# Attention scores built by a transfer through DRAM and VectorE instead of by TensorE

## The reference, cut to what matters

```
first branch (once):   h = x' @ W_fc^T ; f1 = h.a1 ; f2 = h.a2
    s[i,j] = leaky_relu(f1[i] + f2[j], 0.2), -1e9 where adj[i,j] == 0
    out = elu(softmax_j(s) @ x')
second branch (3 layers), mask = adj + eye > 0:
    si = x @ attn_w[l,:256] ; sj = x @ attn_w[l,256:]
    s[i,j] = leaky_relu(si[i] + sj[j] + attn_b[l], 0.2), -inf where not mask
    h = layernorm(x + softmax_j(s) @ x) * g1 + beta1
    x = layernorm(h + gelu(h @ W1 + b1) @ W2 + b2) * g2 + beta2      (W1 256x1024, W2 1024x256)
```

## Time and profile before

| | |
|---|---|
| median of 3 runs | 2795.41 us (2794.3 to 2795.49) |
| the profiled execution | 2794.51 us, of it span 2792.7 us |
| busy share of the span | TensorE 96%, its weight loads 86%, VectorE 82%, ScalarE 77%, GpSimd 61% |
| mean granted TensorE clock | 0.981 of full |
| DMA | 201.34 MB, mean 72 GB/s; queue 1 holds 21.8% of 16 engines' span |

### The profile page before, as it was taken

One profiled execution on the slowest core, in us unless ns is written; L12 is line 12 of the kernel. 1 busy time (PEld: TensorE's weight loads), 2 busy tenths in 40 slices (PEclk: granted clock), 3 DMA queues, 4 the chain that ended last, 5 costly groups with the idle time before them and its releaser, 6 DMA issues.

```text
span 2792.7 us, 53529 instructions
## 1 busy us (share of the span) xinstructions
PE 2668.0 (96%) x16868; PEld 2390.7 (86%) x16868; DVE 2301.8 (82%) x8507; ACT 2147.8 (77%) x3982; POOL 1692.1 (61%) x2197
## 2 busy tenths in 40 slices
PE   3599999999999999999999999999999999999997
PEld 2388989898888898898888898989888999999997
DVE  5999888889888888888888888888988777777774
ACT  4588888878787878787877787878777876776774
POOL 4656655656766565666666665655666644544655
PEclk7599999999999999999999999999999999999999
DMA  6221122212222221222221212121323111111111
GB/s 188 93 75 54 65 76 65 71 61 86 83 96 69 66 73 52 80 65 83 79 97 59 80 65 76 56 80 45 102 80 99 54 52 52 35 52 52 50 63 53
DMA packets 118014, 201.34 MB, mean 72 GB/s; under 512 B 12736, under 2 KB 85472, under 8 KB 117728
## 3 DMA queue, kind: packets, MB, share of 16 engines
q1 hardware_dynamic: 117728, 197.87, 21.8%
HBM read 113.95 MB, written 83.89 MB: 71 GB/s over the span
## 4 chain that ended last, share of the span: by engine, by line
PE 70%; DVE 14%; POOL 7%; issue 5%; ACT 3%; DMA 0%; DVEq 0%; POOLq 0%; SPq 0%; ACTq 0%
PE bank L569 33%; PE bank L554 26%; PE ps_u L528 5%; DVE g_lo L917 3%; DVE st L891 3%; POOL xo L358 3%; PE ps_u L610 2%; PE ps_s L523 2%; POOL rs L1198 2%; DVE ub L972 1%; POOL hb L358 1%; DVE ub L1002 1%; PE ps_s L515 1%; DVE vb L886 1%; ACT g_hi L792 1%
## 5 line engine op out<-in xcount | busy, mean ns | idle before, releaser
L569 PE MATMUL bank<-w_hi,g_hi 128*128 128x256 f32 x3072 | 891.7, 290 | 19.0 <-DVE g_lo L917 18.2
L569 PE MATMUL bank<-w_hi,g_lo 128*128 128x256 f32 x3072 | 865.0, 282 | 0.0
L569 PE MATMUL bank<-w_lo,g_hi 128*128 128x256 f32 x3072 | 863.6, 281 | 0.0
L792 ACT ACTIVATE g_hi<-bank,b_eff 128x512 fp32r<-128x512 f32 x768 | 529.0, 689 | 432.8 <-PE bank L554 427.4
L917 DVE TENSOR_TENSOR g_lo<-bank,g_hi 128x512 fp32r<-128x512 f32 x768 | 517.7, 686 | 178.3 <-ACT bank L794 165.7
L554 PE MATMUL bank<-zt_hi,w_hi 128*128 128x512 f32 x1536 | 646.6, 421 | 7.1 <-DVE g_lo L917 3.7
L554 PE MATMUL bank<-zt_hi,w_lo 128*128 128x512 f32 x1536 | 607.1, 395 | 0.0
L554 PE MATMUL bank<-zt_lo,w_hi 128*128 128x512 f32 x1536 | 606.1, 395 | 0.0
L569 PEld LDWEIGHTS bank<-w_hi,g_hi 128*128 128x128 f32 x3072 | 578.5, 188 | 30.5 <-DVE g_lo L917 29.2
L569 PEld LDWEIGHTS bank<-w_lo,g_hi 128*128 128x128 f32 x3072 | 579.1, 189 | 0.8
L569 PEld LDWEIGHTS bank<-w_hi,g_lo 128*128 128x128 f32 x3072 | 578.3, 188 | 0.0
(11 more groups left out here) (95 smaller groups left out, 4291.7 us busy)
## 6 DMA issues: line engine op xcount, KB each, us to landing
xb<-x_scratch SPq DMA_DIRECT2D x88, 512.0 KB, 4.0
x_scratch<-xo SPq DMA_DIRECT2D x64, 512.0 KB, 4.8
xin<-in_x SPq DMA_DIRECT2D x40, 512.0 KB, 4.6
r_scratch<-elu_r SPq DMA_DIRECT2D x32, 512.0 KB, 3.1
xin<-r_scratch SPq DMA_DIRECT2D x32, 512.0 KB, 4.6
out<-xo SPq DMA_DIRECT2D x32, 512.0 KB, 3.3
m<-m_scratch SPq DMA_DIRECT2D x96, 128.0 KB, 3.7
x_scratch<-h SPq DMA_DIRECT2D x24, 512.0 KB, 2.9
```

The costliest lines, as they stand in the source:

```text
L569: mm = pe.matmul(y, g[:, c, r * P:(r + 1) * P], w[:, l, c, :], start=(c == 0 and n == 0), stop=(c == C - 1 and n == 2))
L792: act.activation(g_hi[:, c, :], block_in, ACT.Gelu, bias=bias).then_inc(g_hi_ready, 1)
```

## The change

For steps from 0 on (`by_memory(s)`), scores no longer pass TensorE. When the dots of a unit are there, SP writes the column `dots[:, 1, :]` to a small DRAM tensor `s2_u` (each element a piece of its own), waits for it, and reads it back as one row of 512 values broadcast over the 128 partitions, straight into `e1` (`e0` for the first branch). VectorE adds the mask and takes the row maximum in one fused instruction per graph, whose output stays in `e1`. ScalarE makes its exponentials from `e1`, one into PSUM and one in place. In steps below 0 the old way stays.

With it come moves: on VectorE `next_biases` goes from behind `first_variance` to behind `g_low(5)`, `input_statistics`, `second_statistics`, `low_rows` and the variances to behind `g_low(7)`; on TensorE `turns` goes from ahead of `second(3)` to behind it; waits on `scores_ready` become waits on `cc_ready`; some semaphores count by other numbers.

```diff
# SP, head of body
+                if by_memory(s) and v1 is not None:
+                    sp.wait_ge(dots0_ready, 2 * T * st.nth0(v1))
+                    sp.wait_ge(masks0_ready, st.nth0(v1))
+                    sp.dma_start(s2_u[2].rearrange("t n -> n t"), dots0[:, 1, :],
+                                 allow_slow_non_contiguous=True).then_inc(s2_0_out, 16 if v1 > V0 else 16 * (V0 + 1))
+                    sp.wait_ge(s2_0_out, 16 * st.nth0(v1))
+                    if v1 <= CH:
+                        sp.wait_ge(et0_ps, st.nth0(v1 - 1))
+                    sp.dma_start(e0.rearrange("p t m -> p (t m)"),
+                                 s2_u[2].rearrange("t n -> (t n)").partition_broadcast(P)).then_inc(s2_0_in, 16 if v1 > V0 else 16 * (V0 + 1))
...
-                        sp.wait_ge(scores_ready, st.nth(s + 1))
+                        sp.wait_ge(cc_ready if by_memory(s - 1) else scores_ready, st.nth(s + 1))
# SP, behind the store of m_new, ahead of the store of elu_r and the load of xin
+                if by_memory(s + 1) and live(s + 3):
+                    sp.wait_ge(dots_ready, st.nth(s + 3, 2 * T))
+                    sp.dma_start(s2_u[(s + 3) % 2].rearrange("t n -> n t"), dots[(s + 3) % 2][:, 1, :],
+                                 allow_slow_non_contiguous=True).then_inc(s2_out, 48 if s + 3 == 2 else 16)
+                    sp.wait_ge(m_in, 16 * st.nth(s + 3))
+                    sp.wait_ge(s2_out, 16 * st.nth(s + 3))
+                    sp.wait_ge(et_ps, st.nth(s + 3))
+                    sp.dma_start(e1.rearrange("p t m -> p (t m)"),
+                                 s2_u[(s + 3) % 2].rearrange("t n -> (t n)").partition_broadcast(P)).then_inc(s2_in, 16)
# TensorE, steps from 0 on
                 hidden(1)
-                next_scores()
                 first_turn()
                 hidden(2)
                 hidden(3)
-                first_scores()
...
                 second(2)
+                second(3)
                 turns()
-                second(3)
# ScalarE, exponentials
+                    if in_e:
+                        act.activation(src, e[:, t, :], ACT.Exp, bias=cols[:, 1, t:t + 1], scale=SLOPE)
+                        a = act.activation(e[:, t, :], e[:, t, :], ACT.Exp, bias=cols[:, 0, t:t + 1])
# VectorE, branch_biases (the scalar step now comes first)
-                dve.tensor_reduce(sm[:, 0, :], scores.rearrange("p (t m) -> p t m", t=T), AX, ALU.max)
+                if mask is None:
+                    ins = dve.tensor_reduce(sm[:, 0, :], scores, AX, ALU.max)
+                else:
+                    for t in range(T):
+                        ins = dve.tensor_tensor_reduce(scores[:, t, :], scores[:, t, :], mask[:, t, :], 1.0, LOWEST,
+                                                       ALU.add, ALU.max, sm[:, 0, t:t + 1])
# VectorE, order of steps from 0 on
                 g_low(1)
                 first_variance()
-                next_biases()
                 g_low(2)
                 first_norm()
                 g_low(3)
-                input_statistics()
                 g_low(4)
                 g_low(5)
+                next_biases()
+                g_low(6)
+                g_low(7)
+                input_statistics()
                 second_statistics()
-                g_low(6)
+                low_rows()
                 second_variance()
-                g_low(7)
                 input_variance()
                 if v1 is not None and early_step(v1) >= 0:
                     mask_sums(v1)
-                low_rows()
                 input_shift()
# GpSimd, first_mask
-                            pool.wait_ge(scores0_ready, st.nth0(v0 - 1))
+                            pool.wait_ge(cc0_ready if by_memory(s) else scores0_ready, st.nth0(v0 - 1))
```

More of the change, by code:

```diff
@@ L18 @@
 BIG = 2.0 ** 100
+LOWEST = -3.0e38
 class Step:
@@ L207, in build @@
         m_in = sem("m_in")
+        s2_out = sem("s2_out")
+        s2_in = sem("s2_in")
+        s2_0_out = sem("s2_0_out")
+        s2_0_in = sem("s2_0_in")
         m_out = sem("m_out")
@@ L450, in body @@
                         sp.dma_start(xb[(s + 3) % 2][:, :, :],
-                                     pick(xs_u, st, layer(s + 3) * G + group(s + 3))).then_inc(x_in, 16)
+                                     pick(xs_u, st, layer(s + 3) * G + group(s + 3))).then_inc(x_in, 16 if s + 3 > CH else 16 * (CH - 2))
                 if live(s - 2):
@@ L583, in next_scores @@
                 def next_scores():
-                    if live(s + 2):
+                    if live(s + 2) and not by_memory(s):
                         pe.wait_ge(dots_ready, st.nth(s + 2, 2 * T))
@@ L596, in first_scores @@
                 def first_scores():
-                    if v1 is not None:
+                    if v1 is not None and not by_memory(s):
                         pe.wait_ge(dots0_ready, st.nth0(v1, 2 * T))
@@ L628, in turns @@
                         pe.wait_ge(e_ready, st.nth(s + 2))
-                        turn_weights(ps_s, e1, et_ps)
+                        turn_weights(ps_s, e1, et_ps, 2 if s + 2 == 0 else 1)
                 if s < 0:
@@ L918, in g_low, with masked, mask_of @@
                                           ALU.subtract).then_inc(g_lo_ready, 1)
+                def masked(e, scores):
+                    return e[:, :, :] if by_memory(s) else scores.rearrange("p (t m) -> p t m", t=T)
+                def mask_of(m):
+                    return m if by_memory(s) else None
                 def first_biases():
                     if v1 is not None:
[L922 to L923 removed]
+                        if by_memory(s):
+                            dve.wait_ge(s2_0_in, 16 * st.nth0(v1))
+                        else:
+                            dve.wait_ge(scores0_ready, st.nth0(v1))
+                        branch_biases(st.nth0, v1, masked(e0, ps_s0), mask_of(m0), small0, dots0, cc0, None, max0_steps, cc0_ready)
                 junk = ub if s >= 0 else vb
@@ L988, in next_biases @@
                     if live(s + 2):
-                        dve.wait_ge(scores_ready, st.nth(s + 2))
+                        if by_memory(s):
+                            dve.wait_ge(s2_in, 16 * st.nth(s))
+                        else:
+                            dve.wait_ge(scores_ready, st.nth(s + 2))
                         if live(s + 1):
@@ L992, in next_biases @@
                         l2 = layer(s + 2)
-                        branch_biases(st.nth, s + 2, ps_s, small, dots[s % 2], cc, ab_col[:, l2:l2 + 1], max_steps,
+                        branch_biases(st.nth, s + 2, masked(e1, ps_s), mask_of(m1[s % 2]), small, dots[s % 2], cc, ab_col[:, l2:l2 + 1], max_steps,
                                       cc_ready)
```

32 lines of the change are left out of this document (19 added, 13 removed).

## The result

The change makes the kernel slower: 3237.86 us median of 4 runs (3234.14 to 3242.39) against 2794.88 of the kernel before on the same chip, ratio 1.158 (95% interval 1.157 to 1.160), +443 us. The forecast had the sign right and the size wrong: 2985 us, range up to 3050.

A forecast was written before the change was run, and what follows sets the result against it. TensorE was taken to bound C and the light steps, VectorE A. Periods of A, B, C gave 154 us, the residual-sum root 13, light steps 24: 191 on 2794.5, so 2985 us, own range 2900 to 3050, stated range 2775 to 3050.

The forecast's parts named there:

- the sign: Whole kernel: slower given 0.75, same 0.07, faster 0.18.
- A: Step s mod 3 = 2, input rows of a new group and norm of an older one: 27.35 to 32.3 us, +4.9.
- B: Step s mod 3 = 0, middle stage of the first branch: 26.9 to 27.4 us, +0.5.
- C: Step s mod 3 = 1, late stage of the first branch: 29.4 us, +1.0.
- the locks: Biases on VectorE beside GpSimd's hb, each operation waiting for a GpSimd instruction: 3.0 us per step, bounds 0 and 3.7.
- Rival 1: Fused operations don't lock against hb: about 2782 us; 0.07 as no change, 0.18 for faster together with another rival.
- light step: One of the 20 last steps, without first branch, bound by TensorE and a link: 26.2 to 27.4 us, +1.2.
- uncovered root in A: VectorE's input_shift follows the variances directly and waits for two roots on GpSimd: 1.5 us.
- Cost 0: SP's write of the dots and the broadcast land well before the biases, 12 us into the step: no cost.
- rival 4: Transfers land later than 12 us; 5 us more would make over 3200 us; chance 0.03.
- TensorE has no idle time at all: In the 20 last steps of 26.22 us TensorE never idles, so it bounds them.
- the 80 of the prediction: Score rows taken off TensorE, 121 x 0.66 = 80 us, the most the change can give.

The follow-up runs named there:

- e1: Kernel after without the 4-byte writes of the dots to DRAM and their waits, broadcasts reading a constant row: 3107.3 us.
- e3: Kernel after without the 4-byte writes (broadcast of a constant row) and with GpSimd's scaled rows (hb) behind the biases: 2935.7 us.
- e7: Kernel after with dots written as 128 pieces of 16 bytes and e1, e0 laid out node by graph, computation complete: 3160.7 us.
- e10: Kernel before with only the statistics, low rows and variances moved behind g_low(7), biases at their old place: 2939.5 us.
- e5: e3 with the turn of the weights again ahead of second(3) on TensorE: 3028.5 us.
- e6: e4 with the turn of the weights again ahead of second(3) on TensorE: 3045.0 us.
- e13: Kernel before without the four transposes of the score rows, the mask's matmul alone writing the bank: 2771.1 us, ratio 0.9915.
- e2: Kernel after with GpSimd's scaled rows (hb) made to wait until the biases of the same step are done: 3070.3 us.
- e4: Kernel after with its orders kept, but scores made by TensorE as before and no transfers through DRAM: 2945.3 us.
- e9: Kernel before with only next_biases moved behind g_low(5) in the steady state: 3097.3 us.
- e12: Kernel after with 16-byte pieces, kernel before's order on VectorE and TensorE, own broadcast tile, first branch left on TensorE: 2835.7 us, ratio 1.0146.

## Why the prediction was right or wrong

**Where the forecast went.** The profiled execution grew by 439 us. Against the forecast, by kind of step: the first five 45 (forecast 0), 23 A 131 (24 A: 118), 23 B 139 (25), 23 C 73 (24), the last 20 steps 51 (24). A came out; B is the largest miss.

**Right: the sign and the locks; A with some luck.** Rival 1 (no locks) is refuted. The pitch of 0.74 us for a held operation, worked out from the dots of a prologue step, is what the trace has (median 0.743 us), though fewer than half of the operations are held. Forecast for locks: 3.0 us of VectorE per step, of which 2.6 came (biases 4.3 us in e1, 1.7 in e3). Measured as a part of the total: 172 us (e1 to e3), 1.7 us per light step, 2.5 in A. The Trainium skill, SBUF — State Buffer, section "Who interferes with whom", calls the port pair that the two engines share an exclusive lock. The prediction's 0.91 us per operation was an estimate from that, and the measurement sides with the smaller figure. The uncovered root in A was forecast with 1.5 us and measured with 1.63. But A's +4.9 was made of 3.0 for locks and 1.9 for the rest, and e1 and e3 have 2.5 and 2.7: two errors that nearly cancel.

**Wrong: the queues.** "Cost 0" for the transfers rested on a row in which 768 pieces of 4 bytes landed in 2.5 us. That transfer went from DRAM to SBUF, and in that direction even 3072 pieces of 4 bytes (`b_col`, 12 KB) landed in 4.4 us; the new one goes from SBUF to DRAM, and SP waits 8.9 to 10.1 us for 512 pieces. That the direction makes the difference is not shown by an edit; e7 shows that larger and fewer pieces in the same direction are fast. I had noted the threshold (12 us for both transfers) and given it 0.03; write plus broadcast (5.3 us median), 14 to 15 us, are above it, and in B two pairs stand in one queue ahead of `xb`. It costs 131 us (e1), half of it (65 us) in B. This is rival 4 at a lower price than it was given, on top of the forecast and not in its place.

**Wrong: the size of the order.** The step that failed is the one that let TensorE alone bound B, C and the light steps, and charged the uncovered roots to A only (and to every third B). Without locks the prediction's rival 1 had A +1.9, B -1.3, C -0.7 and light -0.66; e3, which has neither writes nor locks, gives +2.7, +1.6, -0.3 and +0.2. B is the worst: the shift waits for the roots there too, and the weights come late for the turn, which cost TensorE 1.3 us per B and 4.0 per A in e10, where biases and turn stand at their old places. The prediction had seen that `e_ready` would be late and left it out of the sum. With locks (e1) the steps are +5.2, +2.7, +1.6 and +1.9 against the forecast +4.9, +0.5, +1.0 and +1.2. The chain of a light step in e1 shows a further link that was left out, 3.35 us from the end of the turn (2703.05) to g_lo(0) (2706.40) instead of 2.83:

```profile
2703.69 1.28 ACT L819
2704.99 0.70 ACT g_hi L819
2705.71 0.67 ACT bank L821
2707.01 1.66 DVE ub L1016 x4
```

With the turn behind `second(3)`, ScalarE's copy of it (0.60) and the load of the gelu table (1.28) come after TensorE's step and ahead of the first gelu. The prediction had priced that move at nothing, "if ScalarE is free". The 0.5 us are not its net price: e5 and e6, which undo the move, are slower, because the late weights then hold TensorE.

**Left out: the first steps.** 158.5 to 203.0 us in the first five steps from 0 on, 44 of the 443, of which the writes are 16 and the locks another 16. I extrapolated from the steady state alone.

**Wrong in the premise: "TensorE has no idle time at all" in the light steps.** 96% busy and a step of one unbroken busy row looked like a bound of its own. For B and C it nearly was: e13 gets 0.7 of 0.88 and 0.4 of 0.44 us there. In the light steps it gets 0.16 of 0.44, because the score rows stood where TensorE would otherwise wait for `g_lo`. In this order of work the greatest gain the change could have had is nearer the 24 us of e13 than the 80 of the prediction.

The parts 131 (writes), 172 (locks) and 141 (e3 against before) are steps of one chain of runs, so they make up the 443 by construction. What tests them is e2, where the locks taken away first give 168, and e4, where the order alone gives 150.

## What to carry to other kernels

When two engines hand chunks back and forth, a full busy row does not tell who bounds: take a piece of work out, add nothing, and time it, before paying for its removal. Read the granted clock beside every wait of TensorE: in the light steps of e9 the wait is 2.2 us and the clock costs an estimated 1.5 more. A step moved in a hand-written order is priced by what its engine no longer covers (a root on another engine, a table load) and by what it now stands beside. A transfer's price is read only from a row with the same piece size and the same direction.

## What was not expected of the hardware

- SP waits 8.9 to 10.1 us on average, at most 12.2, for 512 pieces of 4 bytes from SBUF to DRAM; for the same 2 KB in 128 pieces of 16 bytes 1.7 us (112.7/66). 768 pieces of 4 bytes from DRAM to SBUF took 2.5 us.
- The same two-input VectorE operation of 128 columns has means of 293, 522, 589 and 749 ns in e2, after, e1 and e7, by what GpSimd does beside it and by the stride of its input.
- The mean granted TensorE clock between 600 and 2200 us is 1.00 before, in e3 and in e12, but 0.96 after and 0.95 in e5, kernels in which TensorE stands for 2 us and more in many steps. Time at the lower level (1.2 GHz), where the matmuls of the second product follow each other by 0.21 us instead of 0.12, is 105 us before, 333 after, 339 in e5 and 342 in e9. It is a part of the costs above, bounded by the estimates there and not measured apart.
